# Order of SyncE's key writes and key loads: one half's writes, two loads, then the other half's writes

## The reference

```
x  = layernorm(L0_attn_x)                       # 1024 tokens x 512
q  = rope((x @ wq).reshape(b, s, 32, 16))
k  = rope((x @ wk).reshape(b, s, 8, 16))
v  = (x @ wv).reshape(b, s, 8, 16)
scores = einsum('bqhd,bkhd->bhqk', q, repeat(k, 4)) / 4 + causal mask
out = softmax(scores) @ repeat(v, 4) @ wo
x  = L0_attn_x + layernorm(out)
x  = x + layernorm(dense(layernorm(x)) + two of eight low-rank experts)
```

## Time and profile before

| | us |
|---|---|
| three executions | 258.24, 260.05, 263.81 |
| median | 260.05 |
| profiled execution, its time | 258.29 |
| profiled execution, its span | 256.6 |
| PE busy in the span | 207.1 |
| DVE busy | 169.8 |
| ACT busy | 135.3 |
| POOL busy | 118.6 |

### The profile page before, as it was taken

One profiled execution on the slowest core, in us unless ns is written; L12 is line 12 of the kernel. 1 busy time (PEld: TensorE's weight loads), 2 busy tenths in 40 slices (PEclk: granted clock), 3 DMA queues, 4 the chain that ended last, 5 costly groups with the idle time before them and its releaser, 6 DMA issues.

```text
span 256.6 us, 3812 instructions
## 1 busy us (share of the span) xinstructions
PE 207.1 (81%) x1292; PEld 125.6 (49%) x1304; DVE 169.8 (66%) x398; ACT 135.3 (53%) x238; POOL 118.6 (46%) x93
## 2 busy tenths in 40 slices
PE   0599999987878799799939994998299888997760
PEld 0575734443444445344414340146289767885640
DVE  1893437769898867678744514155477988898875
ACT  2241603312148779696527766353174585787771
POOL 8100506524377868695257437830555052323031
PEclk9999999999999999999986999599869999999996
DMA  6995079997983066767411230403310001100113
GB/s 167 372 376 213 4 244 211 281 299 153 246 258 68 1 218 157 149 119 184 71 46 28 64 63 28 84 8 86 84 43 0 3 0 41 45 22 19 41 42 124
DMA packets 34067, 29.89 MB, mean 117 GB/s; under 512 B 3968, under 2 KB 29568, under 8 KB 34048
## 3 DMA queue, kind: packets, MB, share of 16 engines
q1 hardware_dynamic: 34048, 29.65, 43.4%
HBM read 17.19 MB, written 10.09 MB: 106 GB/s over the span
## 4 chain that ended last, share of the span: by engine, by line
PE 27%; DVE 19%; DMA 15%; SPq 13%; issue 12%; POOL 7%; ACT 5%; POOLq 1%; ACTq 0%; DVEq 0%
DMA region_b<-q_scr 5%; DMA rden_bc<-r_scr 4%; PE ps L1083 4%; PE ps L1098 3%; PE ps L998 3%; SPq L370 3%; SPq L368 3%; DVE stats L742 3%; POOL attn_t L483 3%; DMA q_scr<-region_c 3%; PE ps L974 3%; PE ps L988 3%; SPq L310 3%; PE ps L1057 2%; PE ps L1146 2%
## 5 line engine op out<-in xcount | busy, mean ns | idle before, releaser
L916 DVE TENSOR_REDUCE nmax<-ps 128x4 f32<-128x1024 f32 x32 | 39.2, 1223 | 16.8 <-PE ps L1057 16.6
L511 POOL TENSOR_SCALAR_AFFINE_SELECT region_a<-region_a 128x1024 f32<-128x1024 f32 x32 | 35.4, 1110 | 23.3 <-ACT region_a L688 22.9
L1083 PE MATMUL ps<-region_b,kst 98*128 98x512 bf16 x96 | 28.8, 404 | 6.6 <-ACT region_a L685 4.6
L688 ACT ACTIVATE region_a<-ps 128x1024 f32<-128x1024 f32 x32 | 32.7, 1022 | 0.7 <-PE ps L1083 0.6
L685 ACT ACTIVATE region_a<-ps 128x512 f32<-128x512 f32 x32 | 19.2, 600 | 21.3 <-PE ps L1083 20.7
L988 PE MATMUL ps<-region_a,region_c 128*128 128x512 f32 x64 | 29.0, 598 | 0.0
L1098 PE MATMUL ps<-region_a,v_aug 128*32 128x512 f32 x192 | 27.2, 641 | 1.9 <-POOL region_a L511 1.9
L913 DVE TENSOR_REDUCE nmax<-ps 128x4 f32<-128x512 f32 x32 | 21.8, 683 | 7.5 <-PE ps L1041 7.2
L553 ACT ACTIVATE std<-mv,eps_sb 128x1 f32<-128x1 f32 x32 | 9.4, 293 | 31.8 <-DVE mv L743 31.8
L547 ACT ACT_TABLE_LOAD x17 | 21.8, 1283 | 1.1 <-PEq L1243 0.8
L1057 PE MATMUL ps<-kst,region_b 96*128 96x128 bf16 x256 | 20.0, 222 | 1.5 <-DVE nmax L916 0.8
(11 more groups left out here) (105 smaller groups left out, 428.5 us busy)
## 6 DMA issues: line engine op xcount, KB each, us to landing
region_b<-q_scr SPq DMA_DIRECT2D x8, 768.0 KB, 6.5
q_scr<-region_c SPq DMA_DIRECT2D x8, 384.0 KB, 3.4
x_sb<-x SPq DMA_DIRECT2D x8, 256.0 KB, 5.9
q_scr<-region_c SPq DMA_DIRECT2D x8, 256.0 KB, 3.3
attn_t<-o_sb SPq DMA_DIRECT2D x32, 64.0 KB, 2.3
rden_bc<-r_scr SPq DMA_DIRECT2D x8, 256.0 KB, 3.2
out<-region_b SPq DMA_DIRECT2D x8, 256.0 KB, 2.0
kst<-k_scr SPq DMA_DIRECT2D x8, 192.0 KB, 3.1
```

What stands on the lines that cost most here:

```text
L511: pool.affine_select(out=blocks, in_=blocks, compare_op=ALU.is_ge, fill=0.0, base=0, pattern=[[0, 2], [0, REP], [1, P]], channel_multiplie ...
L688: nc.scalar.activation(probs[:, u % PRING, 1:3, :], ps[:, 4:6, :], ACT.Exp, scale=float(HEAD_DIM) ** -0.5).then_inc(exp_done, 1)
L916: nc.vector.tensor_reduce(nmax[:, gi % 2, 1, heads], ps[:, 1:3, :].rearrange("p a (r k) -> p r a k", r=REP), AX.XY, ALU.max, negate=True). ...
L1083: last = nc.tensor.matmul(ps[:, 3 + j, :], kst[0:TROWS, slot, k, kt * P:(kt + 1) * P], qst[0:TROWS, slot, k * REP:(k + 1) * REP, qt * P:(q ...
```

## The change

SP's program wrote the keys part by part, both halves of each, and then issued the loads of groups 0 and 1. It now writes the three parts of half 0, issues those two loads, and then writes the three parts of half 1. Nothing else is altered; the number of transfers, their sizes and the work of all other engines are the same.

```
             load_q(0)
             load_q(2)
             for part in range(PARTS):
-                for half in range(2):
-                    write_k(part, half)
+                write_k(part, 0)
             load_k(0)
             load_k(1)
+            for part in range(PARTS):
+                write_k(part, 1)
             write_q(2)
             load_q(1)
             load_k(2)
```

## The result

The changed kernel took 263.74 us (median of four, 263.03 to 264.74) against 259.14 us (median of four). The ratio is 1.022, with a 95% interval of 1.018 to 1.027: it is slower by about 5.8 us, and whether by over 2% the interval leaves open. One of the four executions before (263.81 us) ran in a slower state of the chip and is left out of the ratio, which is why that difference is larger than the one of the medians, 4.6 us. The execution that was profiled took 264.74 us with a span of 263.0, against 258.29 and 256.6 before. The forecast was 262.4, in a range of 258.3 to 265.8.

A forecast was written before the change was run, and what follows sets the result against it. The bound changes by stage; between 37 and 65 us it is SP's queue, through unit 4's wait for load_q(1). 258.29 + 2.3 (later write_q(2)) + 1.8 (half clock) = 262.4 us, range 258.3 to 265.8.

The forecast's parts named there:

- `load_k(0)`'s wait: SP's queue, ahead of the key loads: idle from about 45.4 to 49.3, 3.9 us where it was 1.33.
- Half 0's landing: Half 0's last key write lands at 49.3 instead of 50.99, 1.7 us earlier; bounds 47.1 to 49.7.
- rival B: Half 0's writes meet no query-load backlog, landing by 46.9; write_q(2) no later; 257.8 to 258.9 us; chance 0.13, shared.
- Half 1's issues: SP's queue behind the key loads: six writes take 4.1 us (3.8 to 4.6), so write_q(2) starts 2.3 us later.
- `write_q(2)` and `load_q(1)`: Transfers before unit 4: 6.64 us to the last landing and 6.11 for the load, unchanged; unit 4 at 67.1.
- Unit 0: Start of PE's attention work: 0.8 us gained from earlier keys, worth nothing by itself since unit 4 waits for load_q(1).
- ACT's wait for half 1: At split_high(3), ahead of units 1 to 3: ACT and DVE wait 0 to 0.7 us, covered by idle time before unit 4.
- TensorE's clock: PE around unit 4: a gap of 2.9 to 3.7 us brings half clock for 4.3 us, costing 1.8 us.
- rival A: PE before unit 4: the gap comes but TensorE keeps 2.4 GHz; 260.6 us; chance 0.22.
- the bound of 2.9: Upper bound on the half clock's cost around unit 4: half of the 5.8 us of low clock from 160.35 on.
- rival C: SP's queue and PE's clock: half 0 at 49.7, dearer issues, longer low clock; 3.0 + 2.9 = 5.9, 264.2 us; chance 0.15.

The follow-up runs named there:

- Experiment 2: Against the kernel before: half 0's six key writes first, half 1's six still ahead of the two key loads; ratio 0.994 to before.
- experiments 3 and 7: Changed kernel with two, respectively four, of half 1's six key writes issued ahead of the two key loads; ratios 1.013 and 0.997 to before.
- Experiment 8: Changed kernel with one wait more: SP lets all of half 1 land before issuing write_q(2); ratio 1.029 to before.
- experiment 1: The changed kernel run again without any edit, with two more executions recorded; ratio 1.025 to before.
- Experiment 5: Changed kernel with half 1's six key writes moved behind write_q(2), ahead of load_q(1); ratio 1.021 to before.
- filler: Changed kernel with 18 more mask matmuls, output unread, on PE between units 3 and 4; 260.68 us, ratio 1.008 to before.
- experiment 4: Changed kernel with 18 unread mask matmuls added on PE between units 3 and 4; 260.68 us against the changed kernel's 264.68 in the same runs.
- experiment 3: Changed kernel with the two largest of half 1's key writes ahead of the key loads, four behind; ratio 1.013 to before.
- two_ahead: Changed kernel with two of half 1's key writes ahead of the key loads, four behind; ratio 1.013 to before.
- order_only: Against the kernel before: key writes ordered half 0 then half 1, all still ahead of the key loads; ratio 0.994 to before.
- loads_by_act: Against the kernel before: half 0's writes, half 1's, then write_q(2) on SP; ACT issues the two key loads; ratio 0.995 to before.
- four_ahead: Changed kernel with four of half 1's key writes ahead of the key loads, the two small ones behind; ratio 0.997 to before.
- wait_half1: Changed kernel with SP waiting for all of half 1 to land before it issues write_q(2); ratio 1.029 to before.
- after_again: The changed kernel once more, unaltered; ratio 1.025 to before.

## Why the prediction was right

**Direction and mechanism held.** The step on which it rests is that `load_k(0)`'s wait grows as the writes that used to fill it are put behind it. The trace has SP idle from 45.68 to 49.37 (forecast 45.4 to 49.3). Experiment 2 shows it from the other side: with no write behind the wait the kernel gets faster, not slower; experiments 3 and 7 show that the start of `write_q(2)` goes by the number of writes behind it (16.09 with four, 14.62 with two, 17.57 with six, 13.86 with none).

**Half 0's landing**, taken from the four first writes of before, was forecast at 49.3 and was 49.35. The Trainium skill's fit for a lone transfer (DMA: Bandwidth & Descriptors, "Anatomy of one DMA") gave an estimate of 46.95 for it. The last write took 4.37 us and not some 2.1: behind this backlog the trace decides against the fit, and rival B falls.

**Half 1's issues** were mis-sized a little: 50.28 to 54.65 is 4.37 us, forecast 4.1. Measured from SP's first row, `write_q(2)` is 2.76 us later, forecast 2.3.

**`write_q(2)` and `load_q(1)`.** The step that failed is "at 54.3 the backlog of half 1 is gone", by which I left 6.64 us as it was. It took 7.66 us, and 7.61 in the second trace. I had divided bytes by the best rate, 374 GB/s, where the windows show some 210, and the last write of half 1 was issued at 53.96 and landed at 56.1. Experiment 8, with a full wait between, brings 6.66 back. With 0.28 us of a longer load, unit 4 was 4.05 us late and not 2.3.

**Unit 0** started at 53.15 without a wait for keys, which was worth nothing, as said. **ACT's wait for half 1** was forecast at 0 to 0.7 us and hidden by the gap. It was nothing in the first trace, where the cast at 56.31 was released by DVE, and cost unit 2 0.45 us in the second execution of experiment 1, where unit 4 still waited for `load_q(1)`. Experiment 5 shows the price when it is not hidden, unit 4 at 69.92 - 37.43 = 32.49 instead of 27.62.

**TensorE's clock** fell, as the forecast had it against rival A. Sized at 1.8 us, it cost 2.47 in the first trace and 1.5 in the second; in the third it cost 2.5 at this place and 2.05 in group 1, together above the bound of 2.9. The filler of experiment 4 removes the fall and nothing else at that place. The longer gap (5.23 us, forecast 2.9 to 3.7) comes from the term above. The fall was read from one stretch of before, about 2 us into it; here it came 3.8 and 5.1 us into a gap of 5.2, later than the end of the gap that I had forecast. That such a gap brings it too is seen once: in the second execution of experiment 3 PE idled 3.60 us, and the clock fell half a microsecond after work had resumed. One reading was off as well: the low clock behind the row at 160.35 ended at 166.4 (0.78 in the window from 166 to 167), so it had lasted 6.1 us and not 5.8, and the upper bound should have been 3.0.

The sum was 2.3 + 1.8 = 4.1 us; the first trace has 4.05 + 2.47 = 6.5. That 263.74 lies inside the range is in part luck: its upper end had been raised for a median above the profiled execution, not for a term left out. The profiled execution, at 264.74, was nearer to rival C's 264.2 than to 262.4. Of C's three reasons, half 0 did not land later, the issues did cost more (4.37 us), and the clock stayed low nearly as long behind the resumption as C had it (5.4 us); the largest difference, the late landing, is in none of the cases. The ratio of 1.022 lies at the edge of the two per cent that I had given a chance of 0.19.

## What to carry to other kernels

A wait in a queue should stand where the queue has nothing ready to issue. Here twelve ready writes filled the time until six of them had landed; put six behind the wait and the queue loses their issue time, while the load that it hurries had nobody who needed it sooner. Ordering the writes by who needs them first, and leaving the waiting loads behind all of them, was faster than both orders (0.994). And a delay is priced with its echo: a gap that grows on TensorE can cost half clock behind it, here 1.5 to 4.6 us on top of 4, different from one execution to the next.

## What the runs showed of the hardware

- The six writes of `write_q(2)`, with four or six of half 1 issued directly ahead of them, needed 7.5 to 7.9 us from the first issue to the last landing (the changed kernel, two_ahead and filler, seven traces), and 6.65 to 6.97 in before, order_only, loads_by_act, four_ahead and wait_half1, with the bytes the same. At the end of those that took longer the transfers' share is about 0.06 for 1 to 2 us; in wait_half1 that tail is missing.
- Half 1's writes behind the two key loads moved 201 to 217 GB/s (after, 53 to 55 us), the key writes of both halves in turn 355 to 383 (before, 46.5 to 50 us). Why is open.
- After the same idle stretch of PE, 5.2 us, the granted clock fell 3.8 us into it in one execution (cost 2.5 us) and 5.1 us into it in the next (cost 1.5 us). After 4.05 us of filler and 1.39 us idle it did not fall, in two traces. It also fell where no long idle stretch stood directly ahead: at 61.4 us and at 78.5 us in the second execution of after_again.
- Six issues from SP took 4.3 us alone, and 7.4 us while ACT issued six of its own.
